# Attention with an exact row maximum: units of one head pair instead of two, sums by two query halves, and the maxima split by GpSimd

## The chip, the cores and the metric

The kernel runs on one core of one Trainium2 chip. The metric is the device time of one execution in microseconds (us). One execution holds a whole four-layer network; the change touches one function that three of the four layers call.

## The reference

A gated decoder of four layers works on x (1 x 1024 x 128) and a context of 6404 rows x 128. Each layer adds tanh(gate) times a cross attention to the context and then tanh(gate) times a feed-forward part; the feed-forward parts differ (experts, quantized, a local transformer of depth 6, top-2 experts). The attentions have 16 heads of width 8. Those of layers 0, 1 and 3 are the plain kind, for example:

```
energy = einsum('mqhd,mkhd->mhqk', q, k) * SCALE
attn = softmax(where(mask == 0, -1e20, energy), axis=3)
out = einsum('mhqk,mkhd->mqhd', attn, v)
```

Layer 2 keeps only the 32 largest scores of each row and uses another function, which the change leaves alone.

## The kernel before, in words

`attend_with_max` computes softmax attention for 16 heads x 1024 queries x 6404 keys (51 tiles of 128 keys, KT). The scores are needed twice. The first time the queries lie on the partitions: TensorE writes rows of scores (`row_fills`, tile `row`, line 919), and VectorE takes their maxima (`search`, line 1045, 494 keys of two heads in each half of one instruction's 128 x 988 elements). When all maxima of a unit are there, VectorE negates them and splits each into three bf16 parts that are written into `place` (`place_tops`, lines 1055 to 1065). TensorE adds these to the queries (`turn`, lines 959 and 961), and ScalarE copies the result to `qb` (`keep_queries`, line 1019), so that the second product gives score minus maximum at once. The second time the keys lie on the partitions: TensorE makes scores of 128 keys x 512 queries for one head (`scores`, line 932; two heads are one pair on two halves of the rows), ScalarE takes the exponential of each (line 1010), and TensorE multiplies by the values with a column of ones (`sums`, line 945: 128 x 9 weights in f32, results in `acc`, each of four heads on its own 32 partitions). At the end of a unit ScalarE copies `acc` out (`keep_sums`, line 1025), TensorE transposes it (`heads`, line 973, in a bank of `row`), and VectorE divides (lines 1071 and 1073).

A unit is G = 4 heads by 512 queries; there are 8 units. A unit's search is 104 reductions (208 counted in halves, FILLS), and its exponentials are 51 tiles x 4. The search runs one unit and LEAD = 20 (10 reductions) ahead of the exponentials, so a stage begins with 114 reductions during which ScalarE has nothing to do, and ends with some 55 tiles without a reduction. Below, a half tile (two exponentials, two scores, one set of sums and, as a rule, one reduction) is called a step; before, a unit has 102 steps.

The order on each engine is written out by hand. TensorE runs for every tile: scores of the second pair, at tile 48 of a unit the turn of the next unit, at tile 2 the heads of the last unit, then sums part 0, a row fill, scores of the next tile's first pair, sums part 1, and the remaining row fills. Three PSUM banks hold scores, two pairs of banks hold rows: a row fill waits for the reduction two before it, and a pair of scores waits for the exponential two before its second slot. SyncE loads keys for the next group but one when a group is done, and queries after each turn.

Of the kernel before, what the change touches and what calls it, by code (L numbers as in the profile page):

```python
# [810 lines left out]
def load_first_keys(sp, first_keys, first_loaded, kst_l, kmask_l):  # L811

    for j in range(2):
        load_key_rows(sp, first_keys[64 * j:64 * j + ROWS, 0, :], kst_l[j], kmask_l, first_loaded)


def attend_with_max(nc, first_keys, first_loaded, kst_l, kmask_l, vst_l, qst, ident, att, tag):

    UNITS = NG * NQC
    QT = QC // P  # L820
    ITEMS = G * QT
    CW = 494
    NC = -(-S2 // CW)
    FILLS = ITEMS * NC
    LEAD = 20
    TURN_AT = 48
    HEADS_AT = 2
    PROBS = 3
    with ExitStack() as ctx:
        m = Memory(nc, ctx, tag)  # L830
        kg = [first_keys, m.sb("kg1", [P, 2, KPAD], BF16)]
        qn = [m.sb(f"qn{i}", [P, 2, QC], BF16) for i in range(2)]
        qb = [m.sb(f"qb{i}", [P, 2, QC], BF16) for i in range(2)]
        v_all = m.sb("v_all", [P, KT, H, VW])
        prob = [m.sb(f"prob{i}", [P, 2, 2, QC]) for i in range(PROBS)]
        zeros, identb = m.sb("zeros", [P, QC], BF16), m.sb("identb", [P, P], BF16)
        partial, neg, rest = m.sb("partial", [P, 2, ITEMS, NC]), m.sb("neg", [P, ITEMS]), m.sb("rest", [P, ITEMS])
        place = m.sb("place", [P, 2 * QT, 2, 64], BF16)
        ob = m.sb("ob", [P, QC])
        rden = m.sb("rden", [P, QT, G, 1])  # L840
        score = [m.ps(f"score{i}", [P, QC]) for i in range(3)]
        acc = m.ps("acc", [P, QC])
        row = [m.ps(f"row{i}", [P, 2, QC]) for i in range(2)]
        qn_loaded = [m.sem(f"qn_loaded{i}") for i in range(2)]
        kg_loaded = [[first_loaded, m.sem("kg_loaded01")], [m.sem(f"kg_loaded1{pair}") for pair in range(2)]]
        cleared, v_loaded = m.sem("cleared"), m.sem("v_loaded")
        scored, slot_out, summed = m.sem("scored"), m.sem("slot_out"), m.sem("summed")
        filled, reduced, split, placed = m.sem("filled"), m.sem("reduced"), m.sem("split"), m.sem("placed")
# [4 lines left out]
        def row_pairs(tile):  # L853

            done = lambda n: min(UNITS * FILLS, FILLS + LEAD + (n * FILLS // KT) // 2 * 2)
            return range(0, done(0), 2) if tile < 0 else range(done(tile), done(tile + 1), 2)

        def heads_before(tile):

            return 0 if tile < KT + HEADS_AT else (tile - HEADS_AT) // KT  # L860

        def bank_use(pair_fill, tile):
            return pair_fill // 2 + heads_before(tile)

        def slot_use(tile, j):

            u, k = tile // KT, tile % KT
            return G * tile + j + 2 * (1 + u + (1 if k > TURN_AT and u + 1 < UNITS else 0))

        def turn_use(u):  # L870
            return 0 if u == 0 else slot_use((u - 1) * KT + TURN_AT, G - 1) + 1

        @block.sync
        def _(sp):
            def load_keys(g, heads=range(G)):
                for j in heads:
                    load_key_rows(sp, kg[g % 2][64 * (j % 2):64 * (j % 2) + ROWS, j // 2, :], kst_l[g * G + j], kmask_l,
                                  kg_loaded[g % 2][j // 2])

            def load_queries(u):  # L880
                g, qc = u // NQC, u % NQC
                for j in range(G):
                    sp.dma_start(qn[u % 2][64 * (j % 2):64 * (j % 2) + ROWS, j // 2, :],
                                 qst[g * G + j, 0:ROWS, qc * QC:(qc + 1) * QC]).then_inc(qn_loaded[u % 2], 16)

            sp.wait_ge(cleared, 3)
            load_queries(0)
            load_keys(0, range(2, G))
            sp.dma_start(v_all[:, :, :, :], vst_l).then_inc(v_loaded, 16)
            load_queries(1)  # L890
            load_keys(1)
            for u in range(UNITS - 2):

                sp.wait_ge(scored, turn_use(u) + 2)
                load_queries(u + 2)
                if u % NQC == 1 and u // NQC + 2 < NG:
                    sp.wait_ge(summed, (u + 1) * KT)
                    load_keys(u // NQC + 2)

        @block.tensor  # L900
        def _(pe):
            def row_fills(tile, pairs):

                for n in pairs:
                    if n % FILLS == 0:
                        u = n // FILLS
                        pe.wait_ge(qn_loaded[u % 2], 64 * (u // 2 + 1))
                        pe.wait_ge(kg_loaded[u // NQC % 2][0], 2 * KEY_LOADS * (u // NQC // 2 + 1))
                    if n % FILLS == FILLS // 2:
                        u = n // FILLS  # L910
                        pe.wait_ge(kg_loaded[u // NQC % 2][1], 2 * KEY_LOADS * (u // NQC // 2 + 1))
                    use = bank_use(n, tile)
                    if use >= 2:
                        pe.wait_ge(reduced, use - 1)
                    for half in range(2):
                        u, item, c = n // FILLS, n % FILLS // (2 * NC), n % (2 * NC) // 2
                        pair, i = item // QT, item % QT
                        rows = slice(64 * half, 64 * half + ROWS)
                        last = pe.matmul(row[use % 2][:, half, 0:CW], qn[u % 2][rows, pair, i * P:(i + 1) * P],  # L919
                                         kg[u // NQC % 2][rows, pair, c * CW:(c + 1) * CW], start=True, stop=True)  # L920
                    last.then_inc(filled, 1)

            def scores(tile, pair):
                u, k = tile // KT, tile % KT
                use = slot_use(tile, 2 * pair)
                if k == 0 and pair == 0:
                    pe.wait_ge(slot_out, turn_use(u) + 2)
                if use >= 2:
                    pe.wait_ge(slot_out, use - 1)
                for half in range(2):  # L930
                    rows = slice(64 * half, 64 * half + ROWS)
                    pe.matmul(score[(use + half) % 3][:, :], kg[u // NQC % 2][rows, pair, k * P:(k + 1) * P],  # L932
                              qb[u % 2][rows, pair, :], start=True, stop=True).then_inc(scored, 1)

            def sums(tile, part):
                u, k = tile // KT, tile % KT
                columns = slice(part * (QC // 2), (part + 1) * (QC // 2))
                if tile == 0 and part == 0:
                    pe.wait_ge(v_loaded, 16)
                if k == 0 and u and part == 0:  # L940
                    pe.wait_ge(ob_ready, u)
                if part == 0:
                    pe.wait_ge(slot_out, slot_use(tile, G - 1) + 1)
                for j in range(G):
                    last = pe.matmul(acc[32 * j:32 * j + VW, columns], v_all[:, k, u // NQC * G + j, :],  # L945
                                     prob[tile % PROBS][:, j // 2, j % 2, columns], start=(k == 0 and part == 0),
                                     stop=(k == KT - 1 and part == 1), skip_group_check=True)
                if part == 1:
                    last.then_inc(summed, 1)

            def turn(u):
# [3 lines left out]
                if use >= 2:  # L955
                    pe.wait_ge(slot_out, use - 1)
                for pair in range(2):
                    slot = score[(use + pair) % 3]
                    pe.matmul(slot[:, :], identb[:, :], qn[u % 2][:, pair, :], start=True, stop=False)
                    for i in range(QT):  # L960
                        last = pe.matmul(slot[:, i * P:(i + 1) * P],  # L961
                                         place[:, pair * QT + i, :, :].rearrange("p s r -> p (s r)"), identb[:, :],
                                         start=False, stop=(i == QT - 1))
                    last.then_inc(scored, 1)

            def heads(u):

                tile = (u + 1) * KT + HEADS_AT
                use = bank_use(row_pairs(tile).start if u + 1 < UNITS else UNITS * FILLS, tile) - 1
                pe.wait_ge(ob_ready, u + 1)  # L970
                pe.wait_ge(reduced, use - 1)
                for i in range(QT):
# [4 lines left out]
            pe.matmul(acc[:, :], zeros[:, 0:P], zeros[:, :], start=True, stop=True).then_inc(acc_zeroed, 1)  # L977
            row_fills(-1, row_pairs(-1))
            turn(0)
            scores(0, 0)  # L980
            for tile in range(UNITS * KT):
                u, k = tile // KT, tile % KT
# [5 lines left out]
                pairs = row_pairs(tile)  # L988
                if tile:
                    sums(tile - 1, 0)  # L990
                row_fills(tile, pairs[:1])
                if tile + 1 < UNITS * KT:
                    scores(tile + 1, 0)
                if tile:
                    sums(tile - 1, 1)
                row_fills(tile, pairs[1:])
            sums(UNITS * KT - 1, 0)
            sums(UNITS * KT - 1, 1)
# [3 lines left out]
        def _(act):  # L1002
            def exponentials(tile):

                for j in range(G):
                    use = slot_use(tile, j)
                    act.wait_ge(scored, use + 1)
                    if tile >= PROBS:
# [1189 lines left out]
```

## Time and profile before

| what | us |
|---|---|
| median of 3 runs | 7952.15 |
| lowest, highest of them | 7946.94, 7953.99 |
| the profiled execution, own time | 7953.99 |
| its span in the profile | 7953.9 |
| VectorE busy | 6492.8 (82%) |
| TensorE busy | 5961.1 (75%) |
| ScalarE busy | 5294.9 (67%) |
| 2496 search reductions, mean duration | 1.175 |
| 4896 exponentials, mean duration | 0.594 |

Consecutive instructions of one engine overlap a little: a duration is counted from start to end, and the distance from start to start in an unbroken row of instructions is shorter. The timeline merges such a row into one line with a count; its length divided by the count, less the overhang of the last, is that distance. "idle before" is the engine's idle time ahead of the instruction, with the one that ended it.

### The profile page before, as it was taken

The page shows a single profiled execution, that of the slowest core. Times are in us where ns is not written, and L with a number is a line of the kernel's source. Part 1 is how long each engine was busy: PE and PEld are TensorE (multiplying, and loading weights), DVE is VectorE, ACT ScalarE, POOL GpSimd, SP SyncE. Part 2 cuts the span into 40 slices and gives each one's busy share as a digit, 9 for nine tenths or more (in the row PEclk, how much of TensorE's full clock was granted, in tenths as well). Part 3 has the DMA queues.
Part 4 walks back from the last instruction along what each step waited for, and adds up shares of the span by engine and source line. Part 5 has one row for each costly group of instructions (what it writes and reads, how often), then busy time and mean ns, then how long its engine had stood idle before and what let it go on. Part 6 is the DMA issues. An engine that isn't in the chain of part 4 may idle for free. (4 is left out here: it accounts for less than half of the span.)

```text
span 7953.9 us, 124573 instructions
## 1 busy us (share of the span) xinstructions
PE 5961.1 (75%) x45261; PEld 1971.2 (25%) x45261; DVE 6492.8 (82%) x11562; ACT 5294.9 (67%) x8777; POOL 718.6 (9%) x394
## 2 busy tenths in 40 slices
PE   5799997599997455534554777768888886899987
PEld 2122222122222111101110111125555542222223
DVE  5999972799993799999997999976556666999934
ACT  3399995099997455534545999965556651799992
POOL 2000000000000000000000000044445540000000
PEclk8699998699999555555556999989889996899998
DMA  7100001300000000000002000000000002000001
GB/s 224 39 18 3 18 2 48 74 4 18 17 3 5 22 9 9 9 8 8 9 4 50 17 7 13 2 30 9 15 15 12 9 9 59 4 17 18 3 2 48
DMA packets 112350, 176.41 MB, mean 22 GB/s; under 512 B 14817, under 2 KB 94725, under 8 KB 106750
## 3 DMA queue, kind: packets, MB, share of 16 engines
q1 hardware_dynamic: 111774, 168.91, 8.2%
q8 instruction: 339, 5.55, 0.3%
q14 instruction: 237, 1.94, 0.1%
HBM read 125.66 MB, written 43.21 MB: 21 GB/s over the span
## 5 line engine op out<-in xcount | busy, mean ns | idle before, releaser
L1045 DVE TENSOR_REDUCE a_partial<-a_row 128x2 f32<-128x988 f32 x2496 | 2740.3, 1175 | 82.6 <-PE a_row L919 79.2
L1010 ACT ACTIVATE a_prob<-a_score 128x512 f32<-128x512 f32 x4896 | 2648.9, 594 | 115.1 <-PE a_score L932 102.2
L945 PE MATMUL a_acc<-a_prob,a_v_all 128*9 128x256 f32 x19584 | 1527.8, 384 | 0.6 <-ACT a_prob L1010 0.6
L522 ACT COPY m_rows<-m_score 128x1536 f32<-128x1536 f32 (+1 forms) x640 | 760.8, 1250 | 847.1 <-DVE m_edge L573 692.2
L581 DVE MAX8 m_cand<-m_rows 128x8 f32<-128x192 f32 x4352 | 1213.9, 332 | 13.2 <-ACT m_rows L522 13.2
L501 PE MATMUL m_score<-m_kb,m_qb 54*128 54x512 bf16 (+1 forms) x1664 | 765.3, 607 | 415.5 <-ACT m_rows L522 349.4
L803 DVE SCALAR_TENSOR_TENSOR a_prob<-a_score,a_prob 128x1024 f32<-128x1024 f32 x816 | 924.8, 1209 | 38.6 <-ACT a_prob L779 38.6
L779 ACT ACTIVATE a_prob<-a_score,a_lower 128x1024 f32<-128x1024 f32 x816 | 865.9, 1111 | 85.3 <-PE a_score L720 34.8
L919 PE MATMUL a_row<-x_first_keys,a_qn 54*128 54x494 bf16 x2496 | 552.9, 440 | 194.1 <-DVE a_partial L1045 187.7
L932 PE MATMUL a_score<-a_qb,a_kg 54*128 54x512 bf16 x2448 | 469.6, 380 | 55.2 <-ACT a_prob L1010 12.2
L720 PE MATMUL a_score<-a_qb,a_kg 54*128 54x512 bf16 x1632 | 318.5, 390 | 255.5 <-DVE a_prob L803 232.4
L919 PE MATMUL a_row<-a_kg,a_qn 54*128 54x494 bf16 x2496 | 478.7, 380 | 25.7 <-DVE a_partial L1045 24.7
L932 PE MATMUL a_score<-a_qb,x_first_keys 54*128 54x512 bf16 x2448 | 471.3, 381 | 15.5 <-ACT a_prob L1010 13.5
L734 PE MATMUL a_acc<-a_prob,a_v_all 128*9 128x512 f32 x3264 | 431.1, 600 | 14.6 <-DMA a_v_all<-vst 7.7
L945 PEld LDWEIGHTS a_acc<-a_prob,a_v_all 128*9 128x9 f32 x19584 | 291.2, 88 | 606.9 <-issue 578.0
L501 PEld LDWEIGHTS m_score<-m_kb,m_qb 54*128 x1664 | 174.8, 122 | 988.5 <-issue 988.5
L1824 ACT ACTIVATE lt_ex<-lt_duo,lt_nmax 96x128 f32<-96x128 f32 x1056 | 283.7, 367 | 122.5 <-DVE lt_nmax L1973 122.5
L1019 ACT CAST a_qb<-a_score 128x512 bf16<-128x512 f32 x48 | 27.2, 587 | 475.1 <-PE a_score L961 474.9
L1973 DVE TENSOR_REDUCE lt_nmax<-lt_duo 96x8 f32<-96x1024 f32 x132 | 161.1, 1221 | 219.1 <-PE lt_duo L1693 219.1
L484 PE MATMUL m_flags<-m_ones,m_flag 128*1 128x1 f32 x130 | 12.2, 163 | 426.9 <-DVE m_flag L552 426.9
L919 PEld LDWEIGHTS a_row<-x_first_keys,a_qn 54*128 54x128 bf16 x2496 | 123.2, 95 | 761.2 <-DVE a_partial L1045 711.4
L1071 DVE RECIPROCAL a_rden<-a_row 128x16 f32<-128x16 f32 x24 | 6.0, 250 | 361.5 <-PE a_row L973 361.5
(312 smaller groups left out, 6351.2 us busy)
## 6 DMA issues: line engine op xcount, KB each, us to landing
kst<-kv_parts SPq DMA_DIRECT2D x48, 384.0 KB, 3.9
vst<-kv_va SPq DMA_DIRECT2D x48, 288.0 KB, 4.2
e_cb<-comb SPq DMA_DIRECT2D x25, 512.0 KB
a_v_all<-vst SPq DMA_DIRECT2D x3, 3672.0 KB
a_kg<-kst SPq DMA_DIRECT2D x36, 306.0 KB
x_first_keys<-kst SPq DMA_DIRECT2D x24, 306.0 KB
a_kg<-kst SPq DMA_DIRECT2D x36, 204.0 KB
qst<-q_parts SPq DMA_DIRECT2D x24, 256.0 KB
```

Of the source, the lines that this page charges most:

```text
L501: last = pe.matmul(score[(half * NCH + c) % 2][:, k - c * CH:k - c * CH + n], qb[par][:, ds(t2 * (2 * P) + half * P, P)], keys[:, k:k + n] ...
L522: act.copy(rows[i][:, c * CH:c * CH + n], score[(i * NCH + c) % 2][:, 0:n]).then_inc(copied, 1)
L581: last = dve.max(cand[i % 2][:, s, :], rows[i % 4][:, s * W:(s + 1) * W])
L720: last = pe.matmul(score[n % SLOTS][:, half, :], kg[u // NQC % 2][rows, pair, k * P:(k + 1) * P], qb[u % 2][rows, pair, :], start=True, st ...
L734: last = pe.matmul(acc[32 * j:32 * j + VW, :], v_all[:, k, u // NQC * G + j, :], prob[tile % PROBS][:, j // 2, j % 2, :], start=(k == 0), ...
L779: act.activation(prob[tile % PROBS][:, pair, :, :], score[(2 * tile + pair) % SLOTS][:, :, :], ACT.Exp, bias=lower[:, 0:1]).then_inc(exped, 1)
L803: dve.scalar_tensor_tensor(out=prob[tile % PROBS][:, pair, :, :], in0=score[n % SLOTS][:, :, :], scalar=0.0, in1=prob[tile % PROBS][:, pai ...
L919: last = pe.matmul(row[use % 2][:, half, 0:CW], qn[u % 2][rows, pair, i * P:(i + 1) * P], kg[u // NQC % 2][rows, pair, c * CW:(c + 1) * CW ...
L932: pe.matmul(score[(use + half) % 3][:, :], kg[u // NQC % 2][rows, pair, k * P:(k + 1) * P], qb[u % 2][rows, pair, :], start=True, stop=Tru ...
L945: last = pe.matmul(acc[32 * j:32 * j + VW, columns], v_all[:, k, u // NQC * G + j, :], prob[tile % PROBS][:, j // 2, j % 2, columns], star ...
L1010: act.activation(prob[tile % PROBS][:, j // 2, j % 2, :], score[use % 3][:, :], ACT.Exp).then_inc(slot_out, 1)
L1045: dve.tensor_reduce(partial[:, u % 2, 2 * item:2 * item + 2, c], row[use % 2][:, :, 0:CW], AX, ALU.max).then_inc(reduced, 1)
```

## The change

It concerns `attend_with_max` and the first load of its keys.

- A unit is one head pair (2 heads) by 512 queries: 16 units of 51 steps, 52 row fills (one at a time, each with its reduction of the same 128 x 988), 102 exponentials. LEAD is 10 row fills.
- TensorE's order in a step is: turn (at step 45), scores of the next step, heads (at step 3), sums of the last step, row fills. At step 0 the sums of the unit before come ahead of the scores. The double row fill falls on step 50.
- `sums` still fills the four groups of 32 partitions of `acc`: two heads times two halves of the queries (tiles 0 and 2, and 1 and 3, of 128 queries), so `acc` is 256 columns wide; each of the two moving operands of a head is now two runs of 128 columns.
- The turn takes one score bank instead of two, and keep_sums, the transposes and the division have half the size, twice as often.
- After the last reduction of a unit VectorE only makes the negated maximum (now 128 x 8 from 128 x 104). The four small operations of the split run on GpSimd, with a semaphore to it (`lowered`) and between them.
- There are 4 buffers of exponentials of one step instead of 3 of one tile. SyncE's loads are by head pair: at the start both query blocks, then the values, then the second pair's keys; later eight instructions per pair.

The core of the diff:

```diff
-    UNITS = NG * NQC
+    HP = H // 2
+    UNITS = HP * NQC
+    STEPS = UNITS * KT
-    FILLS = ITEMS * NC
-    LEAD = 20
-    TURN_AT = 48
-    HEADS_AT = 2
-    PROBS = 3
+    FILLS = QT * NC
+    LEAD = 10
+    TURN_AT = 45
+    HEADS_AT = 3
+    PROBS = 4
...
+                pe.wait_ge(slot_out, slot_use(step, 1) + 1)
+                for part in range(2):
+                    for j in range(2):
+                        g = 2 * part + j
+                        last = pe.matmul(acc[32 * g:32 * g + VW, :], v_all[:, k, u // NQC * 2 + j, :],
+                                         prob[step % PROBS][:, j, :].rearrange("p (i s c) -> p s i c", s=2, c=P)[:, part],
+                                         start=(k == 0), stop=(k == KT - 1), skip_group_check=True)
+                last.then_inc(summed, 1)
...
             turn(0)
-            scores(0, 0)
-            for tile in range(UNITS * KT):
-                u, k = tile // KT, tile % KT
-                scores(tile, 1)
+            scores(0)
+            for step in range(STEPS):
+                u, k = step // KT, step % KT
                 if k == TURN_AT and u + 1 < UNITS:
                     turn(u + 1)
+                if k == 0 and step:
+                    sums(step - 1)
+                if step + 1 < STEPS:
+                    scores(step + 1)
                 if k == HEADS_AT and u:
                     heads(u - 1)
+                if k:
+                    sums(step - 1)
+                row_fills(step, step_fills(step))
...
+        @block.gpsimd
+        def _(pool):
+
+            shift = [place[:, :, :, AUX + 2 * i + 1] for i in range(3)]
+            flat = lambda t: t[:, :].rearrange("p (t s) -> p t s", s=2)
+            pool.wait_ge(cleared, 5)
+            for u in range(UNITS):
+                pool.wait_ge(lowered, u + 1)
+                if u:
+                    pool.wait_ge(scored, turn_use(u - 1) + 1)
+                pool.tensor_copy(shift[0], flat(neg)).then_inc(split, 1)
+                pool.wait_ge(split, 3 * u + 1)
+                pool.tensor_tensor(flat(rest), flat(neg), shift[0], ALU.subtract).then_inc(split, 1)
+                pool.wait_ge(split, 3 * u + 2)
+                pool.tensor_copy(shift[1], flat(rest)).then_inc(split, 1)
+                pool.wait_ge(split, 3 * u + 3)
+                pool.tensor_tensor(shift[2], flat(rest), shift[1], ALU.subtract).then_inc(placed, 1)
```

## Rows read from the trace of the kernel before

**Rows 1.** Page, busy tenths of VectorE in 40 equal slices of the span.

```profile
DVE  5999972799993799999997999976556666999934
```

**Rows 2.** Windows, the three attention stages: PE, PEld, DVE, ACT, POOL busy, clock, DMA.

```profile
195.00:1267.00 1072.00, 970.16 (x9932) 263.71 (x9932) 925.38 (x886) 897.29 (x1657) 0.00 (x0) 0.93 0.07 15
1472.00:2545.00 1073.00, 970.82 (x9936) 263.86 (x9936) 925.84 (x888) 897.24 (x1657) 0.00 (x0) 0.93 0.07 15
6683.00:7749.00 1066.00, 966.95 (x9922) 262.83 (x9922) 921.08 (x883) 896.85 (x1657) 0.00 (x0) 0.93 0.06 15
```

**Rows 3.** Timeline of VectorE, start of layer 0: start, duration, line, count, [idle before].

```profile
190.50 1.03 DVE L1080 MEMSET a_qn<- 128x512 uint32 x2 [5.00 <-PEq L71]
195.76 113.84 DVE L1045 TENSOR_REDUCE a_partial<-a_row 128x2 f32<-128x988 f32 x104 [3.34 <-PE a_row L919]
309.63 0.37 DVE L1055 TENSOR_REDUCE a_neg<-a_partial 128x16 f32<-128x208 f32 x1
325.78 2.48 DVE L1045 TENSOR_REDUCE a_partial<-a_row 128x2 f32<-128x988 f32 x2 [3.93 <-PE a_row L919]
```

**Rows 4.** Timeline of VectorE, one unit of layer 0.

```profile
452.65 98.52 DVE L1045 TENSOR_REDUCE a_partial<-a_row 128x2 f32<-128x988 f32 x90
551.61 0.21 DVE L1059 CAST a_place<-a_neg 128x16 bf16<-128x16 f32 x1
552.41 3.37 DVE L1045 TENSOR_REDUCE a_partial<-a_row 128x2 f32<-128x988 f32 x3
557.95 1.19 DVE L1045 TENSOR_REDUCE a_partial<-a_row 128x2 f32<-128x988 f32 x1 [2.17 <-PE a_row L919]
568.87 2.28 DVE L1045 TENSOR_REDUCE a_partial<-a_row 128x2 f32<-128x988 f32 x2 [0.43 <-PE a_row L919]
571.78 98.52 DVE L1045 TENSOR_REDUCE a_partial<-a_row 128x2 f32<-128x988 f32 x90
```

**Rows 5.** Chain of waits summed, layer 0: waiting <- awaited, us, times, longest.

```profile
DVE a_partial L1045 <- PE a_row L919: 26.5, 19, 3.9
```

**Rows 6.** Timeline of ScalarE, last unit of layer 0.

```profile
1161.93 103.26 ACT L1010 ACTIVATE a_prob<-a_score 128x512 f32<-128x512 f32 x192 [0.37 <-PE a_score L932]
1266.37 0.59 ACT L1025 COPY a_ob<-a_acc 128x512 f32<-128x512 f32 x1 [1.17 <-PE a_acc L945]
```

**Rows 7.** Timeline of TensorE, steady stretch of layer 0.

```profile
500.92 0.38 PE L919 MATMUL a_row<-a_kg,a_qn 54*128 54x494 bf16 x2
501.14 0.38 PE L932 MATMUL a_score<-a_qb,x_first_keys 54*128 54x512 bf16 x2
501.44 0.62 PE L945 MATMUL a_acc<-a_prob,a_v_all 128*9 128x256 f32 x8
502.01 0.38 PE L919 MATMUL a_row<-a_kg,a_qn 54*128 54x494 bf16 x2
```

**Rows 8.** Timeline, a turn, and two sets of sums in a row.

```profile
1147.70 0.38 PE L959 MATMUL a_score<-a_qn,a_identb 128*128 128x512 bf16 x1 [0.78 <-ACT a_prob L1010]
1148.14 0.38 PE L959 MATMUL a_score<-a_qn,a_identb 128*128 128x512 bf16 x1
1148.39 1.07 ACT L1019 CAST a_qb<-a_score 128x512 bf16<-128x512 f32 x2 [0.35 <-PE a_score L961]
...
1264.01 1.05 PE L945 MATMUL a_acc<-a_prob,a_v_all 128*9 128x256 f32 x16
```

**Rows 9.** Groups of GpSimd by shape: busy us, mean ns | idle before.

```profile
L268 POOL COPY kv_va<-kv_valid 128x64 f32<-128x64 f32 x12 | 5.8, 480 | 0.0
L268 POOL COPY kv_va<-kv_valid 128x48 f32<-128x48 f32 x1 | 1.8, 1753 | 0.0
L103 POOL TENSOR_SCALAR_AFFINE_SELECT g_ident<-g_ident 128x128 f32<-128x128 f32 x1 | 0.3, 293 | 0.2 <-POOL g_ident L101 0.2
```

**Rows 10.** Timeline of SyncE and a window: keys of the next group but one.

```profile
566.43 1.53 SPq L136 DMA_DIRECT2D x_first_keys<-kst  x3
...
600.00:610.00 10.00, 10.00 (x116) 2.83 (x116) 10.00 (x10) 10.00 (x20) 0.00 (x0) 1.00 0.01 2
```

More of the change, by code:

```diff
@@ L834, in attend_with_max @@
         v_all = m.sb("v_all", [P, KT, H, VW])
[L835 to L840, printed above, removed]
+        prob = [m.sb(f"prob{i}", [P, 2, QC]) for i in range(PROBS)]
@@ L843, in attend_with_max @@
         row = [m.ps(f"row{i}", [P, 2, QC]) for i in range(2)]
         qn_loaded = [m.sem(f"qn_loaded{i}") for i in range(2)]
-        kg_loaded = [[first_loaded, m.sem("kg_loaded01")], [m.sem(f"kg_loaded1{pair}") for pair in range(2)]]
+        kg_loaded = [first_loaded, m.sem("kg_loaded1")]
         cleared, v_loaded = m.sem("cleared"), m.sem("v_loaded")
         scored, slot_out, summed = m.sem("scored"), m.sem("slot_out"), m.sem("summed")
-        filled, reduced, split, placed = m.sem("filled"), m.sem("reduced"), m.sem("split"), m.sem("placed")
+        filled, reduced, lowered, split, placed = (m.sem("filled"), m.sem("reduced"), m.sem("lowered"), m.sem("split"),
+                                                   m.sem("placed"))
@@ L851, in attend_with_max, with step_fills @@
         block = ctx.enter_context(nc.Block())
[L853 to L865, printed above, removed]
-            u, k = tile // KT, tile % KT
-            return G * tile + j + 2 * (1 + u + (1 if k > TURN_AT and u + 1 < UNITS else 0))
+        def step_fills(step):
+            done = lambda n: min(UNITS * FILLS, FILLS + LEAD + n * FILLS // KT)
+            return range(0, done(0)) if step < 0 else range(done(step), done(step + 1))
@@ L870, in turn_use, with heads_before, bank_use, slot_use @@
+        def heads_before(step):
+            return 0 if step < KT + HEADS_AT else (step - HEADS_AT) // KT
+        def bank_use(fill, step):
+            return fill + heads_before(step)
+        def slot_use(step, j):
+            u, k = step // KT, step % KT
+            return 2 * step + j + 1 + u + (1 if k > TURN_AT and u + 1 < UNITS else 0)
         def turn_use(u):
-            return 0 if u == 0 else slot_use((u - 1) * KT + TURN_AT, G - 1) + 1
+            return 0 if u == 0 else slot_use((u - 1) * KT + TURN_AT, 1) + 1
@@ L901, in _, with row_fills @@
         def _(pe):
-            def row_fills(tile, pairs):
-                for n in pairs:
+            def row_fills(step, fills):
+                for n in fills:
+                    u, i, c = n // FILLS, n % FILLS // NC, n % NC
                     if n % FILLS == 0:
[L906 to L912, printed above, removed]
+                        pe.wait_ge(qn_loaded[u % 2], 32 * (u // 2 + 1))
+                        pe.wait_ge(kg_loaded[u // NQC % 2], 2 * KEY_LOADS * (u // NQC // 2 + 1))
+                    use = bank_use(n, step)
                     if use >= 2:
@@ L915, in row_fills, with scores @@
                     for half in range(2):
-                        u, item, c = n // FILLS, n % FILLS // (2 * NC), n % (2 * NC) // 2
-                        pair, i = item // QT, item % QT
                         rows = slice(64 * half, 64 * half + ROWS)
-                        last = pe.matmul(row[use % 2][:, half, 0:CW], qn[u % 2][rows, pair, i * P:(i + 1) * P],
-                                         kg[u // NQC % 2][rows, pair, c * CW:(c + 1) * CW], start=True, stop=True)
+                        last = pe.matmul(row[use % 2][:, half, 0:CW], qn[u % 2][rows, i * P:(i + 1) * P],
+                                         kg[u // NQC % 2][rows, c * CW:(c + 1) * CW], start=True, stop=True)
                     last.then_inc(filled, 1)
[L923 to L927, printed above, removed]
+            def scores(step):
+                u, k = step // KT, step % KT
+                use = slot_use(step, 0)
+                if k == 0:
+                    pe.wait_ge(slot_out, turn_use(u) + 1)
                 if use >= 2:
@@ L931, in scores, with sums @@
                     rows = slice(64 * half, 64 * half + ROWS)
[L932 to L938, printed above, removed]
+                    pe.matmul(score[(use + half) % 3][:, :], kg[u // NQC % 2][rows, k * P:(k + 1) * P],
+                              qb[u % 2][rows, :], start=True, stop=True).then_inc(scored, 1)
+            def sums(step):
+                u, k = step // KT, step % KT
+                if step == 0:
                     pe.wait_ge(v_loaded, 16)
-                if k == 0 and u and part == 0:
+                if k == 0 and u:
                     pe.wait_ge(ob_ready, u)
[L942 to L949, printed above, removed]
+                pe.wait_ge(slot_out, slot_use(step, 1) + 1)
+                for part in range(2):
+                    for j in range(2):
+                        g = 2 * part + j
[3 more added lines that the diff above has]
+                last.then_inc(summed, 1)
             def turn(u):
@@ L954, in turn @@
                 pe.wait_ge(placed, u + 1)
[L955 to L964, printed above, removed]
+                if use >= 3:
+                    pe.wait_ge(slot_out, use - 2)
+                slot = score[use % 3]
+                pe.matmul(slot[:, :], identb[:, :], qn[u % 2][:, :], start=True, stop=False)
+                for i in range(QT):
+                    last = pe.matmul(slot[:, i * P:(i + 1) * P], place[:, i, :, :].rearrange("p s r -> p (s r)"),
+                                     identb[:, :], start=False, stop=(i == QT - 1))
+                last.then_inc(scored, 1)
             def heads(u):
-                tile = (u + 1) * KT + HEADS_AT
-                use = bank_use(row_pairs(tile).start if u + 1 < UNITS else UNITS * FILLS, tile) - 1
+                step = (u + 1) * KT + HEADS_AT
+                use = bank_use(step_fills(step).start if u + 1 < UNITS else UNITS * FILLS, step) - 1
                 pe.wait_ge(ob_ready, u + 1)
                 pe.wait_ge(reduced, use - 1)
-                for i in range(QT):
+                for i in range(2):
                     last = pe.transpose(row[use % 2][:, 0, i * P:(i + 1) * P], ob[:, i * P:(i + 1) * P], ident[:, :])
@@ L1002, in _, with exponentials @@
         def _(act):
-            def exponentials(tile):
-                for j in range(G):
-                    use = slot_use(tile, j)
+            def exponentials(step):
+                for j in range(2):
+                    use = slot_use(step, j)
                     act.wait_ge(scored, use + 1)
-                    if tile >= PROBS:
-                        act.wait_ge(summed, tile - PROBS + 1)
-                    act.activation(prob[tile % PROBS][:, j // 2, j % 2, :], score[use % 3][:, :],
-                                   ACT.Exp).then_inc(slot_out, 1)
+                    if step >= PROBS:
+                        act.wait_ge(summed, step - PROBS + 1)
+                    act.activation(prob[step % PROBS][:, j, :], score[use % 3][:, :], ACT.Exp).then_inc(slot_out, 1)
             def keep_queries(u):
@@ L1016, in keep_queries @@
                     act.wait_ge(summed, (u - 1) * KT)
-                for pair in range(2):
-                    act.wait_ge(scored, use + pair + 1)
-                    act.copy(qb[u % 2][:, pair, :], score[(use + pair) % 3][:, :]).then_inc(slot_out, 1)
+                act.wait_ge(scored, use + 1)
+                act.copy(qb[u % 2][:, :], score[use % 3][:, :]).then_inc(slot_out, 1)
             def keep_sums(u):
@@ L1024, in keep_sums @@
                     act.wait_ge(att_ready, u)
-                act.copy(ob[:, :], acc[:, :]).then_inc(ob_ready, 1)
+                act.copy(ob[:, :], acc).then_inc(ob_ready, 1)
             act.wait_ge(acc_zeroed, 1)
             keep_queries(0)
-            for tile in range(UNITS * KT):
-                u, k = tile // KT, tile % KT
-                exponentials(tile)
+            for step in range(STEPS):
+                u, k = step // KT, step % KT
+                exponentials(step)
                 if k == TURN_AT and u + 1 < UNITS:
@@ L1038, in _, with search @@
         @block.vector
         def _(dve):
-            def search(tile):
-                for n in row_pairs(tile):
-                    u, item, c = n // FILLS, n % FILLS // (2 * NC), n % (2 * NC) // 2
-                    use = bank_use(n, tile)
+            def search(step):
+                for n in step_fills(step):
+                    u, i, c = n // FILLS, n % FILLS // NC, n % NC
+                    use = bank_use(n, step)
+                    if n % FILLS == 0 and u >= 2:
+                        dve.wait_ge(lowered, u - 1)
@@ L1082, in _ @@
             search(-1)
-            for tile in range(UNITS * KT):
-                u, k = tile // KT, tile % KT
+            for step in range(STEPS):
+                u, k = step // KT, step % KT
                 if k == HEADS_AT and u:
-                    heads(u - 1, bank_use(row_pairs(tile).start, tile) - 1)
-                search(tile)
-            heads(UNITS - 1, UNITS * FILLS // 2 + UNITS - 1)
+                    heads(u - 1, bank_use(step_fills(step).start, step) - 1)
+                search(step)
+            heads(UNITS - 1, UNITS * FILLS + UNITS - 1)
 def project(nc, att, wo, bo, gate, xs, ident, tag):
```

92 lines of the change are left out of this document (36 added, 56 removed).

## The prediction

> **What bounds the kernel now.** I read the page's slices first, to find where the three attention stages lie: VectorE is full in them but for a gap at their ends [rows 1]. Then the windows over the stages: 1072, 1073 and 1066 us, 3211 of the 7953.9 us, alike in every column, with a mean granted clock of 0.93 (the higher of the two levels is 1.0) [rows 2]. So one stage is worked out and taken three times; nothing else of the network is touched.
>
> Then VectorE's timeline. Layer 0's first reduction starts at 195.76. The first 104 take 113.84 us, (113.84 - 0.08)/104 = 1.094 apart [rows 3]. In a later unit 90 reductions take 98.52 without a break, again 1.094 apart [rows 4]: VectorE is saturated there. Around them lie the negation and split, 1.33 us (452.65 + 90 x 1.094 = 551.08 to the next reduction at 552.41), the division, 0.72 us (568.87 + 2 x 1.094 = 571.06 to 571.78), and idle time, 2.17 and 0.43 us of it in rows shown [rows 4]. All idle time before reductions in the stage is 26.5 us in 19 waits, each for TensorE's row fill, 3.34 us of it ahead of the first and 3.93 at the first exponentials [rows 3, 5].
>
> The last reduction of layer 0 ends at 195.76 + 949.5 = 1145.2 (the last negation starts at 1145.27 in the same timeline), and this sum answers for it: 832 x 1.094 = 910.0, seven splits 9.3, six divisions 4.3, idle 26.5 - 3.3 = 23.2, and some 1.4 for 18 broken overlaps of 0.08: 948.2 of 949.5. After it, ScalarE alone sets the time up to the last copy at 1266.37: 121.1 us. There 192 exponentials take 103.26 [rows 6], 0.5375 apart, 1.075 a step.
>
> TensorE has hardly more room: row fill to scores 0.22 (500.92 to 501.14), scores to sums 0.30, sums to the next fill 0.57, which is 1.09 a step while it waits for VectorE [rows 7]; its own minimum is near 1.08. So three engines at 1.094, 1.08 and 1.075 a step run in lockstep, and a delay of one is made good slowly.
>
> **The search's lead and the tail.** Before, 114 reductions precede the first exponential and 110 steps (55 tiles) follow the last reduction. After, 62 precede it: the last search fill falls on step 755 of 816 (62 + 756 x 52/51 reaches 832), and 60 steps follow. VectorE's 832 reductions stay what they are; what goes is 50 steps of ScalarE's tail at 1.075: **-53.8 us**. This is the core of the forecast. The tail also had one turn's two copies (1.07 and 0.35 idle before [rows 8]), a 0.59 copy of acc with its wait, and transposes; each is half as large now, and no more of each lies in the tail: 121.1 - 110 x 1.075 = 2.9 for these; I take **-1.4**.
>
> **VectorE's own work.** The negation alone: the split's four operations start 0.80 before the next reduction (551.61 to 552.41), so 0.53 of the 1.33 is left; from 208 elements in 0.37 [rows 3] to 104 is 0.11 less at the reduction's slope of about 1 ns an element ((1.175 - 0.37)/780, 1.175 by the table): 0.42. Fifteen of them 6.3, against 9.3. A division gets half the elements, but its cost is mostly fixed: 0.64 each, fourteen of them 9.0, against 4.3. Together **+1.7**. So relieving VectorE of the split pays for the more frequent divisions and little more.
>
> **The turn**, the disputed term. Regularly a fill (500.92) is needed by VectorE 0.95 later (452.65 + 45 x 1.094 = 501.87) and takes 0.38 [rows 4, 7]; with 0.05 for the signal VectorE forgives 0.52. Now TensorE puts a turn of 0.44 (1147.70 to 1148.14 [rows 8]) ahead of scores. These scores must wait for the second instead of the first exponential of step 45, since the turn holds the third bank: 0.54 late. ScalarE's copy (0.54) delays the exponentials behind it, thus the next scores another 0.3. So 0.8 late, 0.5 forgiven: 0.3 us idle on VectorE. Before it was up to 2.17 + 0.43, because VectorE's split first blocks the fills and two banks are taken.
>
> To this comes the wait for `placed`, if GpSimd is late. The last search fill is in step 41; its reduction ends 0.95 + 1.17 after it, the negation at 2.45. TensorE reaches the turn three steps and a fill later, 3.28 + 0.22 + 0.42 for the negation: 3.9. So GpSimd has 1.45 us for four small dependent operations. No row has one. From below: 0.1 us each. From above: 1.75 each, the dearest copy there is; others are 0.48 on average for 64 elements and 0.29 for an affine select behind a wait of 0.2 [rows 9]. I take 0.34 and 0.12 for the wait, the nearest in size: 1.84, late by 0.4 to 0.5 us. While TensorE waits, scores, sums and fills queue behind, so lateness counts in full: 0.3 + 0.5 = 0.8 us a turn (bounds 0.2 and, with 0.9 for each operation, 2.5). Fourteen turns lie in VectorE's part: 11.2. With a start stall of 6.6 less 0.8 for the missing second bank, idle is 17.0 against 23.2; broken overlaps are 1.1 more: **-5.1**.
>
> [...]
>
> **Hidden or small.** The first reduction can start earlier: two memsets of 0.5 us are halved [rows 3], as are two others, and two query loads instead of four are awaited: **-1.2**. The last copy, transposes and division are halved: **-0.5**. Keys: eight loads per pair now, half of what is issued at 566.43, which before were done with the queries before 600 (2 GB/s from there on [rows 10]); about 17 us against 41 steps (45 us) until they are needed, SyncE's query loads behind them included. If that cover went, the row fills of a unit would be late. The values are needed 62 instead of 114 reductions after the start, at 68 us; all loads of a stage, first and later, take 0.07 of its 1072 us of the DMA engines [rows 2], 75 us, and the first ones are less than half of them. Sums by two halves: the same eight instructions a step on the same four groups; no price.
>
> Sum per stage: -53.8 - 1.4 + 1.7 - 5.1 - 1.2 - 0.5 = **-60.3**; three: -181. From the profiled execution's own 7953.99 (0.02% above the median of 7952.15) that is 7773, against the median 7771; I say 7772.
>
> **Rivals.**
> (a) GpSimd clearly late, 0.9 to 1.5 us an operation: 2.5 to 5 us a turn, 42 x 1.7 to 4.2 = +71 to +177: 7843 to 7950. For it: the 1.75 row; against it: the 0.29 row. One way to it has half its chance: if VectorE's running reduction held GpSimd off, each small operation would wait out part of 1.17 us, 0.6 on average: +2.4 a turn, 42 x 2.4 = +101, 7873. The Trainium skill, Perfetto Trace Analysis, section Optimizing Scalar/DVE Operations, warns of this: the two share an SBUF read port, so moving work between them might not help; no row here shows both at work at once.
> (b) Slower: the same mechanism beyond its break-even. 60.3/14 = 4.3 us a turn more than my 0.8, a chain of 6.1 us, over 1.5 us an operation. At 1.75 each, 7 us, 5.6 late: 42 x 5.1 = +214, 7986. What speaks for it is one row, the copy of 48 elements.
> (c) Sums by halves are dearer on TensorE, because of the moving runs of 128. Two sets in a row take 1.05 [rows 8], 0.43 a set. TensorE has 0.014 a step to spare, so beyond that each 0.1 us costs 80 us a stage; break-even at +0.09 on a set. A set twice as long: 816 x 0.41 x 3 - 181 = +820, near 8770. Against it: same columns, same groups.
> (d) The split on GpSimd is hidden and turns cost nothing, and the freed overlap is kept: -0.8 x 42 = -34, with cheaper negations about 7725. The case in which the unit size does nothing is excluded only if ScalarE's tail really is a tail, as it is in the trace [rows 6].
>
> **How the numbers follow.** My case (turns of 0.2 to 2.5 us: -25 and +71, and some 10 for the small terms) 0.80, its own range 7737 to 7845; (a) 0.08, 0.04 of it by way of the shared port; (b) 0.03; (c) 0.03; (d) 0.06. The likeliest time is 7772. The range 7725 to 7845 leaves out most of (a), (b), (c) and half of (d). A measurement tells 0.2% (16 us) from no change. Faster by more: 0.93 (mine, (d), 0.07 of (a)); within: 0.02 (the ends of (a) and (b)); slower: 0.05 (0.02 of (b), and (c)).
>
> **What would show it.** Reductions before the first negation 52 and before the first exponential 62, ScalarE starting some 57 us earlier in each stage; last reduction to last copy 66 us instead of 121; reductions 1.094 apart elsewhere; idle before reductions near 17 us a stage plus the first; TensorE's wait for `placed` near 0.5 us a turn. I am wrong if TensorE's step exceeds 1.094, if the turn waits over 2 us for GpSimd, or if a reduction waits for keys.

## The result: 217 us less, 2.7%

| | before | changed |
|---|---|---|
| median, us | 7949.75 | 7732.59 |
| range of 4 runs, us | 7946.94 to 7953.99 | 7727.66 to 7739.41 |
| the profiled execution, us | 7953.99 | 7739.41 |

The ratio is 0.9727, 95% interval 0.9713 to 0.9741. The forecast was 7772 with 7725 to 7845: the time lies in the range, at its fast end, and 39 us are to be explained.

The profile of the changed kernel, first the windows over the three attention stages (columns as in [rows 2]):

```profile
194.00:1195.00 1001.00, 942.17 (x9920) 263.22 (x9932) 925.43 (x879) 895.45 (x1665) 14.12 (x64) 0.96 0.07 16
1395.00:2397.00 1002.00, 939.78 (x9893) 262.63 (x9909) 926.37 (x883) 893.37 (x1661) 14.13 (x64) 0.96 0.07 17
6525.00:7535.00 1010.00, 942.33 (x9921) 263.51 (x9937) 927.13 (x886) 895.46 (x1665) 14.12 (x64) 0.96 0.07 18
```

The mean clock is 0.96 instead of 0.93. TensorE's busy time fell by some 28 us a stage with the same work, and less of it lies at the lower level of the clock: in layer 0 the granted clock is 0.50 from 195 to 334 us before and from 194 to 272 us now, which is the start of the stage up to the first exponentials; after that its mean is 0.99 before and 1.00 now.

VectorE's timeline in layer 0, the start and one unit, against [rows 3, 4]:

```profile
189.38 0.55 DVE L1073 MEMSET a_qn<- 128x256 uint32 x2 [4.81 <-PEq L71]
...
194.50 56.97 DVE L1052 TENSOR_REDUCE a_partial<-a_row 128x2 f32<-128x988 f32 x52 [4.08 <-PE a_row L915]
251.50 0.26 DVE L1058 TENSOR_REDUCE a_neg<-a_partial 128x8 f32<-128x104 f32 x1
...
265.84 1.19 DVE L1052 TENSOR_REDUCE a_partial<-a_row 128x2 f32<-128x988 f32 x1 [3.14 <-PE a_row L915]
...
330.26 42.75 DVE L1052 TENSOR_REDUCE a_partial<-a_row 128x2 f32<-128x988 f32 x39
373.05 0.26 DVE L1058 TENSOR_REDUCE a_neg<-a_partial 128x8 f32<-128x104 f32 x1
373.23 14.74 DVE L1052 TENSOR_REDUCE a_partial<-a_row 128x2 f32<-128x988 f32 x13
387.88 0.20 DVE L1064 RECIPROCAL a_rden<-a_row 128x8 f32<-128x8 f32 x1
...
388.48 42.75 DVE L1052 TENSOR_REDUCE a_partial<-a_row 128x2 f32<-128x988 f32 x39
```

The first negation comes after 52 reductions, 62 precede the first exponentials. Then a unit takes 58.22 us (330.26 to 388.48); 52 x 1.094 are 56.89 of it. The rest, 1.33: 0.31 for the negation (330.26 + 39 x 1.0938 = 372.92 to 373.23), 0.59 for the division, and 0.43 that the merged row of 13 hides: at the regular distance it would last 12 x 1.094 + 1.18 = 14.31, and it lasts 14.74. Small idle times inside such a row are not written out as idle, so its length must be compared with its count. Two units make 116.4 us where one of twice the size took 119.1 (452.65 to 571.78 [rows 4]).

The last negation of the stage, and ScalarE's timeline to its end, against [rows 6]:

```profile
1129.87 0.26 DVE L1058 TENSOR_REDUCE a_neg<-a_partial 128x8 f32<-128x104 f32 x1
```

```profile
1143.79 49.49 ACT L999 ACTIVATE a_prob<-a_score 128x512 f32<-128x512 f32 x92 [0.15 <-PE a_score L928]
1194.01 0.37 ACT L1012 COPY a_ob<-a_acc 128x256 f32<-128x256 f32 x1 [0.74 <-PE a_acc L941]
```

VectorE's part is 1129.87 - 194.50 = 935.4 us (949.5 before), ScalarE's tail 64.1 (121.1). From the first reduction to the last copy this stage takes 999.5 us, and each of the other two 999.1, instead of 1070.2 to 1070.6. Three stages: -213 of the -215 between the two profiled executions.

A turn, the disputed place (timeline of all engines behind the negation at 373.05; the matmul with the identity that begins the turn is not in the record):

```profile
373.38 0.22 POOL L1035 CAST a_place<-a_neg 128x8 bf16<-128x8 f32 x1 [57.05 <-DVE a_neg L1058]
...
373.68 0.21 POOL L1037 TENSOR_TENSOR a_rest<-a_neg,a_place 128x8 f32<-128x8 f32 x1
373.95 0.22 POOL L1039 CAST a_place<-a_rest 128x8 bf16<-128x8 f32 x1
374.25 0.23 POOL L1041 TENSOR_TENSOR a_place<-a_rest,a_place 128x8 bf16<-128x8 f32 x1
374.46 0.10 PEld L915 LDWEIGHTS a_row<-a_kg,a_qn 54*128 54x128 bf16 x2 [0.67 <-DVE a_partial L1052]
...
375.01 0.39 PE L955 MATMUL a_score<-a_identb,a_place 128*128 128x128 bf16 x4 [0.16 <-issue]
...
376.20 0.38 PE L915 MATMUL a_row<-a_kg,a_qn 54*128 54x494 bf16 x2
```

GpSimd's four operations take 0.21 to 0.23 us each with 0.06 to 0.09 between them, 1.10 from 373.38 to 374.48. TensorE's last fill before the turn is at 374.46. So the split is there when this turn wants it. The waits summed over the whole kernel say nearly the same: the turn's weight loads waited 6.1 us for GpSimd in all, in 19 of 45 turns, 0.9 us at the longest.

```profile
PEld a_score L953 <- POOL a_place L1041: 6.1, 19, 0.9
```

### The profile page after: what moved, and what is told of

Its sections match the earlier page's. It is cut to its first block and busy times, and to the rows that moved or that the text cites. A ratio compares the mean times of both kernels' runs of the same rounds, so it can differ in the third digit from the quotient of the medians.

```text
span 7737.3 us, 125006 instructions
## 1 busy us (share of the span) xinstructions
PE 5876.2 (76%) x45211; PEld 1969.7 (25%) x45261; DVE 6490.5 (84%) x11538; ACT 5289.3 (68%) x8801; POOL 759.4 (10%) x586
## 5 line engine op out<-in xcount | busy, mean ns | idle before, releaser
L915 PE MATMUL a_row<-x_first_keys,a_qn 54*128 54x494 bf16 x2496 | 517.6, 412 | 105.6 <-DVE a_partial L1052 98.0
L1911 POOL TENSOR_TENSOR lt_ex<-lt_ex,lt_rinv 96x1024 f32<-96x1024 f32 x132 | 250.0, 1894 | 352.5 <-DVE lt_rinv L1975 352.5
```

## The experiments

The ratios are to the kernel before on the same chip. Each kernel is the changed one with the edit shown, unless said otherwise.

**Does it matter where the split is?** The four operations go back to VectorE, behind its negation:

```diff
-        @block.gpsimd
...
+                        dve.wait_ge(lowered, u + 1)
...
+                        dve.tensor_copy(shift[0], flat(neg)).then_inc(split, 1)
...
+                        dve.tensor_tensor(shift[2], flat(rest), shift[1], ALU.subtract).then_inc(placed, 1)
```

> The changed kernel with the four split operations moved back to VectorE, everything else as changed. My theory: they lie on the saturated engine, so each unit pays the 0.80 us that they took there before, 14 units in VectorE's part of a stage, three stages: +34 us on the changed kernel's 7733, so 7767, ratio to before 0.977; VectorE idle at a turn stays 0.3 us. Rival: as in the kernel before, the block of VectorE also starves TensorE, its clock falls to the lower level for some 3 us, and a turn costs 1.5 to 2 us more: +34 + 63 to 84, 7830 to 7850, ratio 0.985 to 0.988. Second rival: the split's place does not matter, ratio 0.973.

Measured: 7770.48 us, ratio 0.9771 (0.9755 to 0.9788), against 0.9727 (0.9713 to 0.9741) of the change; the medians differ by 38 us. VectorE's timeline, and the windows around the turn:

```profile
373.89 0.26 DVE L1043 TENSOR_REDUCE a_neg<-a_partial 128x8 f32<-128x104 f32 x1
374.19 0.19 DVE L1047 CAST a_place<-a_neg 128x8 bf16<-128x8 f32 x1
374.41 0.17 DVE L1049 TENSOR_TENSOR a_rest<-a_neg,a_place 128x8 f32<-128x8 f32 x1
374.62 0.19 DVE L1051 CAST a_place<-a_rest 128x8 bf16<-128x8 f32 x1
374.84 0.20 DVE L1053 TENSOR_TENSOR a_place<-a_rest,a_place 128x8 bf16<-128x8 f32 x1
374.93 14.74 DVE L1037 TENSOR_REDUCE a_partial<-a_row 128x2 f32<-128x988 f32 x13
389.58 0.20 DVE L1059 RECIPROCAL a_rden<-a_row 128x8 f32<-128x8 f32 x1
```

```profile
373.00:376.00 3.00, 2.14 (x24) 0.53 (x23) 2.83 (x7) 2.62 (x5) 0.00 (x0) 1.00 0.02 5
376.00:379.00 3.00, 2.63 (x28) 0.95 (x29) 2.97 (x4) 1.81 (x4) 0.00 (x0) 1.00 0.00 0
```

The next reduction starts 1.04 us after the negation instead of 0.18, and the row of 13 behind it is again 14.74 long. So the split costs its own length on the saturated engine, 0.86 a unit (14 x 3 x 0.86 = 36), and nothing at the turn. The rival with the fall of the clock did not come: the granted clock stays 1.00 there.

**What does a late split cost?** One subtraction is repeated four times:

```diff
-                pool.wait_ge(split, 3 * u + 1)
-                pool.tensor_tensor(flat(rest), flat(neg), shift[0], ALU.subtract).then_inc(split, 1)
-                pool.wait_ge(split, 3 * u + 2)
+                pool.wait_ge(split, 7 * u + 1)
+                for again in range(5):
+                    pool.tensor_tensor(flat(rest), flat(neg), shift[0], ALU.subtract).then_inc(split, 1)
+                    pool.wait_ge(split, 7 * u + 2 + again)
```

> The changed kernel with one of GpSimd's subtractions repeated four more times with the same result, each behind the one before it: GpSimd's chain grows from 1.10 us by 4 x 0.29 to about 2.3. It measures what lateness of the split costs. My theory: TensorE waits in its turn some 0.95 us, all that queues behind it is late, and it counts nearly in full, 15 turns by three stages: +38 to +43 us, ratio 0.978. Rival: the 0.5 us that VectorE forgives and ScalarE's own slack take most of it: below +20, ratio at most 0.975.

Measured: 7777.33 us, ratio 0.9779 (0.9763 to 0.9795), 45 us above the median of the change. The turn in the timeline, and the same line of the waits:

```profile
372.53 0.22 POOL L1035 CAST a_place<-a_neg 128x8 bf16<-128x8 f32 x1 [56.81 <-DVE a_neg L1059]
...
372.83 1.35 POOL L1038 TENSOR_TENSOR a_rest<-a_neg,a_place 128x8 f32<-128x8 f32 x5
...
375.06 0.39 PE L955 MATMUL a_score<-a_identb,a_place 128*128 128x128 bf16 x4 [1.06 <-POOL a_place L1042]
...
376.68 2.48 DVE L1053 TENSOR_REDUCE a_partial<-a_row 128x2 f32<-128x988 f32 x2 [0.93 <-PE a_row L915]
```

```profile
PEld a_score L953 <- POOL a_place L1042: 53.1, 45, 2.0
```

The wait for GpSimd is 53.1 us in 45 turns instead of 6.1 in 19: 1.0 us more a turn for a chain of 1.17 us more. VectorE idles 0.93 us in one piece where the change had 0.31 in small ones, and a unit of layer 0 lasts 59.12 us (329.42 to 388.54) instead of 58.22. So a chain 1.17 us longer makes TensorE wait 1.0 us more and a unit 0.90 us longer: the delay is paid nearly in full, and the rival fell.

**Is the gain the shorter lead?** LEAD 30 instead of 10:

```diff
-    LEAD = 10
+    LEAD = 30
     TURN_AT = 45
```

> The changed kernel with LEAD 30 instead of 10: 82 reductions ahead of the first exponential, 80 steps after the last search fill instead of 60. My theory (the gain is the shorter lead and tail): 20 steps by 1.075 us by three stages, +64 us, ratio 0.981; the units' turns unchanged. Rival (the gain is in the smaller turns and divisions, not in the lead): within 10 us of the changed kernel, ratio 0.973.

Measured: 7796.44 us, ratio 0.9806 (0.979 to 0.9823), 64 us above the change. VectorE's last negation of the stage, and ScalarE's last copy:

```profile
1127.97 0.26 DVE L1058 TENSOR_REDUCE a_neg<-a_partial 128x8 f32<-128x104 f32 x1
```

```profile
1213.44 0.37 ACT L1012 COPY a_ob<-a_acc 128x256 f32<-128x256 f32 x1 [0.74 <-PE a_acc L941]
```

The tail is 85.5 us, 21.4 more than with LEAD 10; VectorE's part, from a first reduction at 192.90, is 935.1 us against 935.4. Each step of lead costs 64/20 = 3.2 us over the three stages. The change saves 50 of them, 160 us by this slope; that is an estimate, since no run changes the size of the unit alone.

**A shorter lead still.** LEAD 6 with the turn at step 49:

```diff
-    LEAD = 10
-    TURN_AT = 45
+    LEAD = 6
+    TURN_AT = 49
```

> The changed kernel with LEAD 6 and the turn at step 49 instead of 45 (the same four steps between last search fill and turn): 56 steps after the last search fill. My theory: 4 x 1.075 x 3 = 13 us less, ratio 0.971. Rival: the turn now meets the double fill at step 50 and the copy of the sums at step 0, and each unit loses 0.5 us more, 45 units: +22 - 13, ratio 0.974.

Measured: 7720.49 us, ratio 0.9712 (0.9695 to 0.9728). That interval overlaps the change's, so both were run once more beside each other, five times each:

> The changed kernel as it is, beside the other runs of this call, so that they can be compared with it on one chip. Ratio to before 0.973.

> LEAD 6 with the turn at step 49 once more, beside the changed kernel. My theory: 12 us below it, ratio 0.9712 against 0.9727, and the difference is real. Rival: the first difference of 12 us was between two chips or calls; then both are within 5 us here.

Measured: 7736.15 us, ratio 0.9728 (0.9714 to 0.9741), for the change, and 7715.11, ratio 0.9704 (0.969 to 0.9717), for LEAD 6. Twice lower, by 12 and 21 us, where 13 were expected. The intervals of the ratios still touch, but the five times of LEAD 6 (7711.81 to 7721.64) all lie below the five of the change (7724.10 to 7736.75). The traces show the same: in layer 0 of the first run a unit lasts 58.19 us against 58.22, so the later turn costs nothing, and the tail is 59.8 us (1128.57 to 1188.41) against 64.1, four steps less. It is the fastest version here.

**The split in the kernel before.** The kernel before, with its units of two pairs, gets only the split on GpSimd:

```diff
-                dve.wait_ge(split, 4 * u + 1)
...
-                dve.tensor_tensor(shift[2], flat(rest), shift[1], ALU.subtract).then_inc(placed, 1)
+        @block.gpsimd
...
+                pool.tensor_tensor(shift[2], flat(rest), shift[1], ALU.subtract).then_inc(placed, 1)
```

> The kernel before, with units of two head pairs, but with the four split operations on GpSimd as in the change. My theory: 0.80 us off VectorE in 7 units by three stages, -17 us; and the fills no longer stop for the split ahead of the turn, so that TensorE does not idle and keeps its clock: VectorE's idle time of 2.8 us around a turn falls to 1.3, another -27 us; together 7906, ratio 0.9945. Rival: the turn's two banks and the wait for an exponential ahead of it make that idle time and the fall of the clock: only -17 us, ratio 0.998. Second rival: GpSimd late for 16 values a row instead of 8, no gain.

Measured: 7913.46 us, ratio 0.9955 (0.994 to 0.997), 40 us less than before. VectorE's timeline of one unit, to be read against [rows 4] and the row of the kernel before that stands first here:

```profile
559.57 8.88 DVE L1045 TENSOR_REDUCE a_partial<-a_row 128x2 f32<-128x988 f32 x8 [0.43 <-PE a_row L919]
```

```profile
446.91 98.53 DVE L1064 TENSOR_REDUCE a_partial<-a_row 128x2 f32<-128x988 f32 x90
545.48 0.37 DVE L1074 TENSOR_REDUCE a_neg<-a_partial 128x16 f32<-128x208 f32 x1
545.76 3.37 DVE L1064 TENSOR_REDUCE a_partial<-a_row 128x2 f32<-128x988 f32 x3
550.32 9.96 DVE L1064 TENSOR_REDUCE a_partial<-a_row 128x2 f32<-128x988 f32 x9 [1.19 <-PE a_row L920]
560.70 2.28 DVE L1064 TENSOR_REDUCE a_partial<-a_row 128x2 f32<-128x988 f32 x2 [0.43 <-PE a_row L920]
...
563.62 98.53 DVE L1064 TENSOR_REDUCE a_partial<-a_row 128x2 f32<-128x988 f32 x90
```

The negation blocks VectorE for 0.28 us (545.48 to 545.76), where the negation and the split took 1.21 (551.20 to 552.41). The idle time behind it is 1.19 instead of 2.17 + 0.43, with another 0.43 ahead of the division in both, and a unit lasts 116.71 instead of 119.13. The windows around the turn, the kernel before and then this one:

```profile
553.00:556.00 3.00, 1.57 (x13) 0.79 (x14) 2.78 (x3) 1.39 (x4) 0.00 (x0) 0.93 0.00 0
556.00:559.00 3.00, 3.00 (x24) 0.53 (x22) 1.05 (x1) 1.52 (x4) 0.00 (x0) 0.50 0.00 0
```

```profile
547.00:550.00 3.00, 2.23 (x24) 0.99 (x26) 2.13 (x2) 2.32 (x5) 0.15 (x1) 1.00 0.00 0
550.00:553.00 3.00, 3.00 (x36) 0.74 (x33) 2.68 (x3) 2.61 (x6) 0.00 (x0) 1.00 0.04 8
```

In the kernel before, TensorE is busy for 1.57 of 3 us ahead of the turn, and then the granted clock is 0.50 for 3 us: the lower level, at which the same eight matmuls of sums last 1.04 instead of 0.62 us in the timeline. With the split on GpSimd it stays at 1.00.

The blocked fills and the fall of the clock can be told apart, because one turn in each stage of the kernel before keeps its clock. In layer 0 it is the turn at 793:

```profile
690.88 98.52 DVE L1045 TENSOR_REDUCE a_partial<-a_row 128x2 f32<-128x988 f32 x90
...
795.20 9.95 DVE L1045 TENSOR_REDUCE a_partial<-a_row 128x2 f32<-128x988 f32 x9 [1.19 <-PE a_row L919]
...
808.50 98.53 DVE L1045 TENSOR_REDUCE a_partial<-a_row 128x2 f32<-128x988 f32 x90
```

The clock is 1.00 in all windows from 787 to 799, the split is on VectorE, and the idle time behind it is 1.19, just as with the split on GpSimd. That unit lasts 117.62 us. So the split's own length costs 0.91 us a unit (117.62 against 116.71), and the fall of the clock 1.5 us (119.13 against 117.62). Of the 18 regular turns of the three stages, 15 fall to the lower level, with 2.5 to 2.7 us idle on VectorE behind them, and none of the 18 with the split on GpSimd. That makes 21 x 0.91 + 15 x 1.5 = 42 us, for 40 measured. So the first theory, with 44 us, is right in the main. Of the rival this much holds: 1.19 us are idle at the turn whatever the split does. That they come from the turn's two banks was not tested apart.

**Do the two runs of 128 columns cost anything?**

```diff
-                                         prob[step % PROBS][:, j, :].rearrange("p (i s c) -> p s i c", s=2, c=P)[:, part],
+                                         prob[step % PROBS][:, j, part * (QC // 2):(part + 1) * (QC // 2)],
```

> The changed kernel with the two query halves of the sums as queries 0 to 255 and 256 to 511, each one run of 256 columns, instead of two runs of 128. This leaves the second and third block of 128 queries exchanged in the output; the work is the same. My theory: the runs cost nothing, ratio 0.973. Rival: a second run costs the sums some time; TensorE's step has only 0.014 us to spare, so this would show as over 10 us less, ratio below 0.9715.

Measured: 7732.42 us, ratio 0.9725 (0.971 to 0.974), the change's own. TensorE's timeline in a regular step, this kernel and then the changed one:

```profile
501.52 0.38 PE L928 MATMUL a_score<-a_qb,x_first_keys 54*128 54x512 bf16 x2
501.83 0.62 PE L941 MATMUL a_acc<-a_prob,a_v_all 128*9 128x256 f32 x8
502.38 0.38 PE L915 MATMUL a_row<-x_first_keys,a_qn 54*128 54x494 bf16 x2
```

```profile
401.20 0.38 PE L928 MATMUL a_score<-a_qb,a_kg 54*128 54x512 bf16 x2
401.51 0.62 PE L941 MATMUL a_acc<-a_prob,a_v_all 128*9 128x256 f32 x8
402.06 0.38 PE L915 MATMUL a_row<-a_kg,a_qn 54*128 54x494 bf16 x2
```

Scores to sums 0.31 and sums to fill 0.55 in both, against 0.30 and 0.57 in the kernel before [rows 7].

## Why the prediction was right, and where it missed

**What bounds the kernel** held. Reductions are 1.094 apart wherever nothing interrupts them, and ScalarE alone sets the tail.

**The lead and the tail**, forecast -53.8 and -1.4 a stage, measured 121.1 - 64.1 = 57.0. The main term was right, and lead_30 shows it as a slope: 3.2 us a step against 3 x 1.075. The rest was 1.8 too low. With 0.5375 taken off for each exponential, ScalarE's copies and waits in the tail come to 4.4 us before and 2.4 now, 2.0 less where 1.4 was put down, and counted from the last negation the tail is 51 steps shorter, not 50.

**VectorE's own work**, forecast 0.42 for a negation and 0.64 for a division, measured 0.31 and 0.59. The next reduction overlaps the negation (0.18 from start to start, 0.26 long), which had not been counted.

**The turn** is the step whose size was off. Forecast: 0.3 us for the third bank and ScalarE's copy and 0.5 for a late GpSimd. Measured: 0.43 in all between negation and division. By single instructions most of it is behind the turn: the reductions at 375.42 and 377.92 are 2.50 apart instead of 2.19, which is 0.31 us; the rest lies at the copy of the sums. So the 0.3 was right, and of the 0.5 next to nothing was there: 6.1 us in 45 turns, 0.14 a turn. GpSimd had been priced at 0.34 and 0.12 for each operation, 1.84 for four, near the rows of an affine select on 128 elements (0.29 behind a wait of 0.2) and a copy of 64 (0.48); it took 1.10, against a budget that was right (1.45 forecast; from the negation's end at 373.31 to some 0.2 after the fill at 374.46 it is 1.4). Rows of 48 and more elements were too large a likeness for 8. The mechanism behind the 0.5 is real, though: with 1.17 us more in the chain (pool_longer), TensorE waits 1.0 us more.

The Trainium skill, GPSIMD Engine Reference, section 3.1 (Elementwise), says that to do elementwise work on VectorE "stays the rule". The runs here differ, and VectorE is the bound in them: with the four operations on it (split_vector) the kernel is slower by 0.4%.

The sum of it: per stage VectorE's part was forecast 3.4 us shorter and came 14.1 shorter. Of these 10.7 us, 7.4 are 14 units at 1.33 instead of 1.86, some 2 are overlaps that were counted as broken and were not, and 1 is not accounted for. The tail was forecast 55.2 shorter and came 57.0 shorter. Three times 12.5 are 37 us. The start of a stage, forecast 1.2 shorter, came so in two stages and not in layer 0: from the first memset to the first reduction 5.12, 3.72 and 3.64 us instead of 5.26, 5.11 and 5.19, in all 3.1 against 3.6. The query loads wait for the memsets and are issued 0.84 instead of 1.59 us after the first, in every stage; in layer 0 they then took longer to land. The 37 us and the 34 between the forecast 7773 and the profiled 7739 so agree within 3.

**The rivals.** (a) and (b), a late GpSimd: its mechanism is real, in pool_longer 1.0 us a turn cost 45 us; its condition is not met, since the chain took 1.10 us. The way over a shared port, which the Trainium skill, Perfetto Trace Analysis, section Optimizing Scalar/DVE Operations, warns of, is not seen: while GpSimd works (373.38 to 374.48), VectorE's reductions start at 373.23 and 374.32, 1.09 apart, and GpSimd's operations take 0.22 beside a running reduction. (c), dearer sums, fell: scores to sums to fill takes 0.86 in the change and 0.87 before. (d) came nearest, and the measured 7733 lies closer to its 7725 than to the forecast 7772: the split costs next to nothing. It had taken the turn as free too, and of that 0.3 us remained.

**Where 217 us come from.** The lead, 50 steps by 3.2: 160 us, by the slope of lead_30. The split, 0.86 us a unit, 42 units: 36 us, run as split_vector. The remaining 20 us were not run apart. In the traces the 15 falls of the clock at a turn, 1.5 us each, are gone (22 us), in split_vector as well; the smaller work in the tail and the earlier start give some 9 more, and the more frequent negations and divisions take some of it back. In the kernel before, the split cost 40 us with half as many units, because some 22 of the 40 us are falls of the clock. Whether the one-bank turn or the four steps between negation and turn keeps the clock up in the changed kernel with the split on VectorE was not separated.

## What to carry to other kernels

When one engine must run ahead of another by a whole unit of work, the unit shows twice, as one engine idle at the start and the other idle at the end, and is paid once: the time is the first engine's whole work plus the second one's tail. Halving the unit saves half of its length, here 50 steps or 54 us a stage, if the fixed work per unit, now done twice as often, stays small beside that. A small serial chain can leave the saturated engine for a slow one if the steps between producer and consumer are counted: here 1.10 us fitted into 1.4, while a chain of 2.3 cost 45 us, more than the 38 that moving it had saved. In a lockstep of three engines within 2%, a wait in the in-order queue of the one in the middle was paid nearly in full: 1.0 us more of waiting made a unit 0.90 us longer.

## What was not expected of the hardware

Four dependent GpSimd operations on 128 x 8 take 1.10 us with their semaphores, 0.22 each, where VectorE takes 0.17 to 0.20 each. And a stop of TensorE can cost more than itself, or not: in the kernel before it waits 1.20 us ahead of a fill and 0.78 ahead of the turn (553.65, 555.02), and 3 us at the lower clock follow; at the turn at 793 it waits 1.19 and 0.77 (791.88, 793.25), and the clock stays at 1.00. The first happened in 15 of 18 turns, the second in 3; what decides between them, no run here shows. With waits of 0.27 and 0.77 (the split on GpSimd) or one of 1.02 (split_vector) the clock stayed up.
